# Writing the first quad's score stacks straight from the parts in an attention kernel

## The reference

```python
xn = _layernorm(x, axis=-1)
Q, K, V = split_heads(xn @ wq.T), split_heads(xn @ wk.T), split_heads(xn @ wv.T)   # 16 heads of 8 channels
Q, K = _rope(Q, THETA), _rope(K, THETA)
scores = jnp.einsum('bhqd,bhkd->bhqk', Q, K) / sqrt(8)      # causal mask, softmax
out = (softmax(scores) @ V) @ wo.T
x = x + out + (xn @ CB.T) * (SCB / 127) + bias
```

## Time and profile before

| | |
|---|---|
| median of 3 runs | 259.69 us (259.62 to 261.62) |
| the profiled execution's own time | 259.88 us |
| its span, first to last instruction | 258.2 us |
| TensorE busy | 240.1 us, 93% |
| VectorE busy | 218.7 us, 85% |
| ScalarE busy | 183.6 us, 71% |
| GpSimd busy | 103.6 us, 40% |
| mean DMA rate | 89 GB/s |

### The profile page before, as it was taken

One profiled execution on the slowest core, in us unless ns is written; L12 is line 12 of the kernel. 1 busy time (PEld: TensorE's weight loads), 2 busy tenths in 40 slices (PEclk: granted clock), 3 DMA queues, 4 the chain that ended last, 5 costly groups with the idle time before them and its releaser, 6 DMA issues.

```text
span 258.2 us, 10150 instructions
## 1 busy us (share of the span) xinstructions
PE 240.1 (93%) x4294; PEld 124.1 (48%) x4294; DVE 218.7 (85%) x594; ACT 183.6 (71%) x360; POOL 103.6 (40%) x169
## 2 busy tenths in 40 slices
PE   6888896888999999999999999999999999999945
PEld 6546541233344555554554465445555554436334
DVE  7899268999999999989999998999889989962072
ACT  2045732273997888779788878889889799999701
POOL 7570724749856391293233032304401430440300
PEclk9999998699999999999999999999999999999997
DMA  7625758620230467162027103700770210010602
GB/s 196 220 66 150 202 120 156 144 46 4 67 85 23 106 165 129 44 165 67 5 81 165 29 4 103 158 18 3 192 163 5 90 41 4 3 44 20 182 10 84
DMA packets 23559, 22.96 MB, mean 89 GB/s; under 512 B 2757, under 2 KB 20549, under 8 KB 23513
## 3 DMA queue, kind: packets, MB, share of 16 engines
q1 hardware_dynamic: 23368, 22.05, 34.3%
q10 hardware_dynamic: 144, 0.26, 0.4%
HBM read 13.70 MB, written 8.39 MB: 86 GB/s over the span
## 4 chain that ended last, share of the span: by engine, by line
PE 72%; DVE 13%; ACT 5%; DMA 4%; SPq 2%; issue 2%; POOL 1%; ACTq 0%
PE psA L918 22%; PE psB L918 20%; PE psV L990 18%; DVE prod L802 8%; ACT ring L697 3%; PE psB L906 2%; PE psB L901 2%; PE psA L1030 2%; DMA qs<-shiftsT 2%; SPq L384 2%; DMA rest<-o_scratch 2%; PE psA L872 1%; DVE rest L815 1%; PE psB L872 1%; ACT xnT L639 1%
## 5 line engine op out<-in xcount | busy, mean ns | idle before, releaser
L802 DVE CUSTOM_DVE_ANT_0 prod<-psA,cmask 128x128 f32<-128x128 f32 (+7 forms) x256 | 177.9, 754 | 16.7 <-PE psA L918 15.6
L697 ACT ACTIVATE ring<-psB 128x512 f32<-128x512 f32 x288 | 154.5, 608 | 33.6 <-PE psB L918 30.7
L918 PE MATMUL psB<-qs,ks 128*32 128x512 bf16 (+3 forms) x1536 | 99.2, 327 | 0.5 <-DMA qs<-shiftsT 0.2
L918 PE MATMUL psA<-ks,qs 128*32 128x512 bf16 (+3 forms) x1536 | 94.7, 334 | 5.3 <-DVE mx L802 4.5
L990 PE MATMUL psV<-ring,va 128*32 128x512 f32 (+3 forms) x768 | 76.0, 486 | 0.1
L918 PEld LDWEIGHTS psB<-qs,ks 128*32 128x32 bf16 x1536 | 40.8, 96 | 48.6 <-ACT ring L697 24.2
L559 POOL TENSOR_SCALAR_AFFINE_SELECT ring<-ring 128x512 f32<-128x512 f32 x64 | 40.0, 642 | 48.2 <-ACT ring L697 48.2
L918 PEld LDWEIGHTS psA<-ks,qs 128*32 128x32 bf16 x1536 | 34.2, 96 | 43.8 <-DVE mx L802 28.0
L539 POOL CAST shifts<-mx 128x16 bf16<-128x16 f32 x16 | 3.2, 198 | 71.0 <-DVE mx L802 71.0
L990 PEld LDWEIGHTS psV<-ring,va 128*32 128x32 f32 x768 | 22.5, 110 | 16.6 <-issue 8.9
L802 DVE DVE_READ_ACCUMULATOR2_ANT mx<- 128x1 f32 x256 | 21.3, 83 | 0.0
(11 more groups left out here) (89 smaller groups left out, 157.0 us busy)
## 6 DMA issues: line engine op xcount, KB each, us to landing
qs<-q_scratch SPq DMA_DIRECT2D x48, 96.0 KB
ks<-k_scratch SPq DMA_DIRECT2D x48, 96.0 KB
o_scratch<-ot SPq DMA_DIRECT2D x12, 256.0 KB, 2.6
q_scratch<-ot SPq DMA_DIRECT2D x20, 128.0 KB, 2.5
k_scratch<-ot SPq DMA_DIRECT2D x12, 128.0 KB, 2.5
x_sb<-x SPq DMA_DIRECT2D x4, 256.0 KB, 4.5
rope_sb<-rope SPq DMA_DIRECT2D x2, 512.0 KB, 6.8
rot<-o_scratch SPq DMA_DIRECT2D x3, 256.0 KB, 3.5
```

What stands on the lines that cost most here:

```text
L697: act.activation(ring[:, s % P_RING, k * HALF:(k + 1) * HALF], bank_b(e % B_RING), ACT.Exp)\
L802: last = dve.tensor_tensor_reduce(masked_scores[:, u % 2, at:at + w], psA[:, (u % 2) * SEQ + at:(u % 2) * SEQ + at + w], cmask[:, SEQ - w: ...
L918: mm = pe.matmul(psum[strip:strip + STRIP, at:at + size], keys[:, strip:strip + STRIP], queries, start=True, stop=True)
```

## The change

- Quad 0's stacks no longer go through HBM. SP issues, for each of the 12 parts of token halves 0 and 1, three DMAs from the part's first 32 partitions (in SBUF) to 8 rows each of the stack (in SBUF): 36 DMAs of 32 KB (`stack_part`). They stand ahead of everything else on SP after the inputs; the 16 stores of `store_parts(0)` and `store_parts(1)` come behind them, then the loads for quads 1 and 2.
- For that the channels are ordered by quad, then dimension, then head (the host permutes the weights' rows and the rope table), so that the 32 partitions of a quad, read in order, are 8 dimensions of 4 heads. The scratch tensors get the shape [quads, parts, dimension, head, tokens].
- Two tasks stand ahead of quad 0's first unit instead of five, and all 22 units of quad 0 stand ahead of bank 0. The third and the fourth group of four tiles of the normalised x are made on ACT (`normalise(2)`, `normalise(3)`) with a bias that POOL computes.
- ACT issues the two DMAs of quad 0's shifts itself. `load_stack(3)` moves between `store_shifts(1, 1)` and `store_parts(3)`.
- All tables are new.

```diff
-        scratch = (nc.dram_tensor("q_scratch", [HEADS, PARTS + 2, DH, BATCH * SEQ], BF16),
-                   nc.dram_tensor("k_scratch", [HEADS, PARTS, DH, BATCH * SEQ], BF16))
+        scratch = (nc.dram_tensor("q_scratch", [HEADS // QUAD, PARTS + 2, DH, QUAD, BATCH * SEQ], BF16),
+                   nc.dram_tensor("k_scratch", [HEADS // QUAD, PARTS, DH, QUAD, BATCH * SEQ], BF16))
...
-                    sp.dma_start(scratch[c % 2][:, m, :, tok:tok + HALF], part(c, n)).then_inc(scratch_out[c // 2], 16)
+                    sp.dma_start(scratch[c % 2][:, m, :, :, tok:tok + HALF], part(c, n)).then_inc(scratch_out[c // 2], 16)
...
-                                     source[heads, first:first + PARTS, :, tok:tok + HALF]
-                                     .rearrange("h p d t -> (p d) h t")).then_inc(ready, 16)
+                                     source[i % 4, first:first + PARTS, :, :, tok:tok + HALF]
+                                     .rearrange("p d h t -> (p d) h t")).then_inc(ready, 16)
...
+            def stack_part(c, n):
+
+                hf, stack = c // 2, (qs, ks)[c % 2]
+                if n < 2:
+                    sp.wait_ge((part1, part2)[n], c + 1)
+                else:
+                    sp.wait_ge(part3[c], 1)
+                for g in range(PARTS):
+                    row = g * GROUP + ((n - g) % PARTS if c % 2 == 0 else n) * DH
+                    sp.dma_start(stack[row:row + DH, 0, hf, :, :], part(c, n)[0:QUAD * DH, :]).then_inc(stack_in[0][hf], 16)
+
+            sp.wait_ge(pads0_ready, 2)
+            for n in range(PARTS):
+                for c in (0, 1):
+                    stack_part(c, n)
+            stack_part(2, 0)
+            stack_part(2, 1)
+            stack_part(3, 0)
+            stack_part(3, 1)
+            stack_part(2, 2)
+            stack_part(3, 2)
             store_parts(0)
-            sp.wait_ge(pads0_ready, 2)
-            sp.wait_ge(scratch_out[0], 16 * ROUND_DMAS)
-            load_stack(0, 0)
             store_parts(1)
+            sp.wait_ge(pads1_ready, 2)
+            sp.wait_ge(scratch_out[0], 16 * ROUND_DMAS)
+            load_stack(1, 0)
             sp.wait_ge(scratch_out[1], 16 * ROUND_DMAS)
-            load_stack(0, 1)
-            sp.wait_ge(pads1_ready, 2)
-            load_stack(1, 0)
             load_stack(1, 1)
-            store_shifts(0, 0)
             sp.wait_ge(pads2_ready, 2)
             load_stack(2, 0)
             load_stack(2, 1)
-            store_shifts(0, 1)
...
+            def first_leave(c):
+                pool.wait_ge(part1, c + 1)
+                pool.wait_ge(part3[c - 2], 1)
+                pool.tensor_tensor(rest[:, c % 2, :], rot[:, c % 2, :], part(c, 0), ALU.subtract).then_inc(rest1, 1)
...
+            def normalise(g):
+                act.wait_ge(shift_ready, g - 1)
+                for t in range(4 * g, 4 * g + 4):
+                    act.activation(xn[:, t, :], x_sb[:, t, :], ACT.Identity, bias=mean_shift[:, t:t + 1],
+                                   scale=rstd[:, t:t + 1]).then_inc(xn_late_ready, 1)
...
-PROJECT_BANK = [269, 276, 296]
-TURN_FIRST = 292
+PROJECT_BANK = [261, 271, 296]
+TURN_FIRST = 285
```

More of the change, by code:

```diff
@@ L435, in _ @@
                 if i == 1:
+                    sp.wait_ge(b_filled, ring_place(i, 0))
+                    load_stack(i + 2, 0)
+                    load_stack(i + 2, 1)
                     store_parts(3)
@@ L439, in _ @@
                         store_heads(done, hf)
-                if i + 2 < QUADS:
+                if 1 < i and i + 2 < QUADS:
                     if i == 2:
@@ L481, in _, with scales, mean_shifts @@
             pads(qs, 1, 0.0, pads1_ready)
-            for g in range(4):
+            def scales(g):
                 bt = slice(4 * g, 4 * g + 4)
-                pool.wait_ge(ln_step, 2 * g + 2)
-                pool.tensor_scalar(var_eps[:, bt], mv[:, bt, 1], EPS, None, ALU.add).then_inc(rstd_step, 1)
-                pool.wait_ge(rstd_step, g + 2)
+                pool.wait_ge(ln_step, 3 * g + 3)
+                pool.wait_ge(rstd_step, 1)
                 pool.tensor_tensor(rstd[:, bt], var_eps[:, bt], exponent[:, bt], ALU.pow).then_inc(rstd_ready, 1)
+            def mean_shifts(g):
+                bt = slice(4 * g, 4 * g + 4)
+                pool.wait_ge(rstd_ready, g + 1)
+                pool.tensor_tensor(mean_shift[:, bt], mv[:, bt, 0], rstd[:, bt], ALU.mult).then_inc(shift_step, 1)
+                pool.wait_ge(shift_step, g - 1)
+                pool.tensor_scalar(mean_shift[:, bt], mean_shift[:, bt], -1.0, None, ALU.mult).then_inc(shift_ready, 1)
+            scales(0)
+            scales(1)
+            scales(2)
+            mean_shifts(2)
             pool.memset(cmask[:, :], 0.0).then_inc(cmask_ready, 1)
@@ L604, in masks @@
                         copy_v(i, 1)
[L605 to L612, removed]
+                if i == 1 and 3 <= s < 7:
+                    add_ffn(s - 3)
+                if i == 2 and 3 <= s < 7:
+                    add_bias(s - 3)
+            beside(-3)
+            pads(qs, 2, 0.0, pads2_ready)
+            pads(ks, 2, TWO_MINUS_ONES, pads2_ready)
+            for n in (-2, -1):
                 beside(n)
@@ L666, in save_task @@
                 last.then_inc(task_saved, 1)
+            def normalise(g):
[3 more added lines that the diff above has]
+                                   scale=rstd[:, t:t + 1]).then_inc(xn_late_ready, 1)
             turned_rows(0)
+            parts_of(0, 0)
             turned_rows(1)
-            for n in range(2):
-                parts_of(0, n)
-                parts_of(1, n)
+            parts_of(1, 0)
+            parts_of(0, 1)
+            parts_of(1, 1)
+            normalise(2)
+            parts_of(2, 0)
             turned_rows(2)
+            parts_of(2, 1)
+            parts_of(3, 0)
             save_task(0)
+            parts_of(3, 1)
+            for n in range(1, ROWS3_FIRST):
+                save_task(n)
+            normalise(3)
             turned_rows(3)
[L676 to L681, removed]
+            for n in range(ROWS3_FIRST, len(TASKS)):
                 save_task(n)
@@ L743, in statistics @@
                 last.then_inc(ln_step, 1)
+                dve.wait_ge(ln_step, 3 * g + 2)
+                bt = slice(4 * g, 4 * g + 4)
+                dve.tensor_scalar(var_eps[:, bt], mv[:, bt, 1], EPS, None, ALU.add).then_inc(ln_step, 1)
             def normalise(g):
@@ L772, in rotate @@
                 cols = slice((r % 2) * HALF, (r % 2 + 1) * HALF)
-                dve.wait_ge(projected, c + 1)
-                for m in range(2):
-                    dve.tensor_tensor(prod[:, c % 2, m, :], round_bank(r, 2 * w + m), rope_sb[:, m, cols],
-                                      ALU.mult).then_inc(products, 1)
+                dve.wait_ge(projected, 2 * c + m + 1)
+                dve.tensor_tensor(prod[:, c % 2, m, :], round_bank(r, 2 * w + m), rope_sb[:, m, cols],
+                                  ALU.mult).then_inc(products, 1)
+            def rotate(c):
                 dve.wait_ge(products, 2 * c + 2)
@@ L781, in rotate, with third_part @@
                                   ALU.add).then_inc(rotated, 1)
-            rotate(0)
-            rotate(1)
+            def third_part(c):
+                dve.wait_ge(part2, c + 1)
+                dve.tensor_tensor(part(c, 2), rest[:, c % 2, :], part(c, 1), ALU.subtract).then_inc(part3[c], 1)
+            for c in (0, 1):
+                product(c, 0)
+                product(c, 1)
+                rotate(c)
             leave(0)
             leave(1)
-            normalise(2)
-            dve.wait_ge(part2, 2)
-            dve.tensor_tensor(part(1, 2), rest[:, 1, :], part(1, 1), ALU.subtract).then_inc(part3[1], 1)
-            normalise(3)
+            product(2, 0)
+            third_part(1)
+            product(2, 1)
             rotate(2)
+            product(3, 0)
+            product(3, 1)
             rotate(3)
-            leave(2)
-            leave(3)
+            statistics(3)
             def maximum(i, u):
```

119 lines of the change are left out of this document (71 added, 48 removed), and 30 rows, old and new, of tables (UNIT_BANK, VALUE_BANK).

## The result

The changed kernel takes **278.01 us** (median of 4 runs, 275.94 to 279.76), the kernel before 259.66: a ratio of 1.068, with an interval of 1.059 to 1.078. The forecast of 268.1 had the sign and the main cause, but less than half of the size: 18.3 us were lost, not 8.2, and the time lies above the range, which ended at 273. The profiled execution took 278.58 us.

What follows compares the result with a forecast made beforehand. TensorE's work was taken to bound the kernel from quad 1's unit 0 to the end of the values, with DVE setting quad 0's pace; 259.88 + 9.9 + 0.9 - 2.6 gave 268.1 us, range 255.5 to 273.

Steps and rivals of the forecast that it cites:

- Stores on four engines: 16 stores ahead of quad 1's loads: four engines, 49 ns per 1 KB, 1.57 us each, 25.1 us in all.
- Rival (b): Stores keep 16 engines: 255.9 us (chance 0.12), or 248.7 us with cheap issues too (chance 0.08).
- (a): Stores on four engines, but the new stack DMAs issue like loads, 0.38 us: 260.9 us; chance 0.20.
- Issue of the new DMAs: Quad 0's stack DMAs on SP: 0.60 us each plus 0.04 between, 36 taking 23.0 us, SP through at 37.7.
- Quad 1's unit 0: First unit of quad 1, behind the stores and six loads: issued at 67.2 us, 9.9 later than at 57.27.
- part three: Everything besides quad 1's unit 0: +0.9 us for work left over, -2.6 in the tail, 0 for shifts and later stores.
- up to 1 us: Stores of rounds 2 and 3: 0, or up to 1 us if the shift of quad 1's second half comes late.
- Half clock after the wait: TensorE returns at half clock after waiting more than 10 us, for up to 6.9 us: +3.4 us at most.
- rival (c): Worse than the forecast: stores at 60 ns a packet, +6.1, so 274 us, or TensorE at half clock; chance 0.10.
- Part one: Start and quad 0: 36 new DMAs, first 640-wide maximum at about 39.8 us, later tasks hidden by DVE's units.
- part two: Stores ahead of quad 1's loads: on four engines, last store at 64.8 us, quad 1's unit 0 at 67.2.
- Tail: After the last value step: quad 7's first-half save stands at bank 18 instead of 23, -2.6 us.

Runs made afterwards that it cites:

- pair of runs above: Changed kernel with its stores on sixteen engines, 260.95 us (ratio 1.006); kernel before with its stores on four engines, 276.09 us (1.064).
- the run with the old pattern: Changed kernel, its stores still on four engines, with loads of stacks reading the scratch in the order of the kernel before: 284.86 us (1.098).
- stores16: Changed kernel with each store going to 128 consecutive scratch rows, so on sixteen engines (also called the sixteen-engine version): 260.95 us (1.006).

## Why the prediction was wrong, step by step

- **Stores on four engines: right.** 80 GB/s and a share of 0.25 were forecast, 96 and 0.27 measured. One packet took 46 ns where 49 were taken (32 × 49 = 1.57 us a store; the sixteen went from 40.1 to the first load that waits for them, at 64.58, in 24.5 us where 27.1 were forecast). The pair of runs above makes the shape alone 16 to 17 us. Rival (b), sixteen engines, is ruled out. (It is also the case meant where the prediction writes "with 16 the sum would be the first rival's": (a) has four engines.)
- **Issue of the new DMAs: right in kind, a little low.** 0.71 for each and not 0.64; SP was through at 40.1 instead of 37.7. Rival (a), at the loads' price, was far off.
- **Quad 1's unit 0: 67.2 forecast, 69.33 measured.** +2.4 from the issues, -2.6 from the stores, and +2.3 from the loads: 2.4 us had been priced by packet counts at 49 ns, and 4.75 us passed between 64.58 and 69.33. The dearer issue of a load isn't the reason, as the run with the old pattern had unit 0 at 68.84. That the number came within 2.1 us is in part luck: misses of both signs.
- **The step that failed** is in part three: "the shifts of quad 0 on ACT's queue ... end long before they are wanted, under the waits above: 0", with the stores of rounds 2 and 3 at "0, with up to 1 us". The stage from quad 1's unit 0 to quad 2's bank 0 was to grow by 0.9 and grew by 11.3. Of this 2.1 us are the work left over (stores16), and 9.2 go with the four-engine stores. Within the 9.2, waits for shift DMAs are 4.9 us of TensorE's idle time, and TensorE's busy time is 52.7 against 48.3 us for the same matmuls: 4.4 us at the lower clock, granted 0.92 on average. The prediction asked which wait ends last at unit 0, and then took everything behind it as the work that it was before. But the late stores had moved quad 1's and quad 2's loads onto the very stretch in which quad 0's second shift is sent, and the shift's packets moved only 3.4 us after its issue, behind them (2.5 us of TensorE's idle time). The next wait, 2.1 us at 106, is the one that "up to 1 us" stood for: the shift is issued at 100.19, behind the last three stores of a round, and lands 5.94 later. That both waits come from the stores' shape is shown by the sixteen-engine version, which has neither; that the second is due to those three stores is my reading.
- **Half clock after the wait** was rival (c)'s: "+3.4 at most". The 4.4 above are of that kind. It isn't a case apart, but comes with the waits: with 9 us of an idle TensorE the granted clock is 0.54 on average over 62.9 to 73.1 us, which is mostly the level of 1.2 GHz; in the sixteen-engine version, without the waits, it is 1.00 throughout the stage.
- **Part one had the later tasks "hidden by DVE's units": they aren't.** In the version without the stores' wait, from the first 640-wide maximum to quad 1's unit 0 pass 18.0 us (42.2 to 60.3), and 17.2 when the stack comes early (31.9 to 49.0, granted clock 1.00). Before it was 15.2 (42.05 to 57.27). TensorE is the one that is full there, not DVE:

```profile
41.70:60.30 18.60, 18.42 (x189) 9.02 (x189) 14.90 (x31) 5.57 (x11) 10.27 (x9) 0.91 0.50 165
```

  Seven tasks among the units cost 2 to 3 us. In the changed kernel this lay beneath the stores' wait, as the prediction said of part two; its rival (b) had unit 0 at 55.0, and of the 5.3 us to the 60.3 that was measured this is about half, the later start (42.2 for 39.8) the rest.
- **Tail: right in mechanism, low in size.** -4.4 us in the changed kernel, and 3.1 us of the whole time in the kernel before (ratio 0.988), against -2.6.

Summed in the prediction's terms: +12.1 for +9.9, +11.0 for +0.9 (11.3 less 0.3), and -4.4 for -2.6.

What stays open is the stretch of the loads' packets to 125 ns, and whether a layout exists that serves quad 0 with few DMAs and lets the stores keep sixteen engines; the sixteen-engine versions here permute the rows of the scratch tensors, and such a layout wasn't tried. Sixteen engines alone wouldn't do: with 36 DMAs on SP those stores only bring back the time before.

## What to carry to other kernels

When a change makes transfers late, price the next stage as well: list every small transfer issued while the late ones drain, and count what was issued ahead of it, by other engines too. Look at the outermost size of each DMA that a new layout touches, on both sides, before anything else: here 4 in place of 16 cost 16 to 17 us, where all the other edits together moved the time by 1.3. And an issue made cheaper is no gain by itself; issuing sooner what isn't urgent puts it ahead of what is.

## What the runs showed of the hardware

- The same load of 24 × 4 rows of 1 KB takes SP 0.376 or 0.758 us to issue, by the order of its rows in HBM alone, in both kernels.
- A DMA from 32 partitions to 8, SBUF to SBUF, takes mostly 0.65 to 0.67 us to issue, and the next one starts about 0.04 behind it.
- A shift DMA of 32 rows of 256 B on two engines lands in 2.0 us with little ahead of it, and in 6.1, 8.6 and 12.9 us among the loads for quads 1 and 2. Its packets start 0.9, 3.4 and 9.4 us after the issue in the runs with 2.0, 6.1 and 12.9: a DMA issued by ACT waits behind what SP issued earlier.
- A 1 KB packet of a load takes about 54 ns where SP's pace sets the rate and 73 ns in a backlog at 162 GB/s; where the loads were issued behind stores on four engines it takes about 125, at 105 GB/s. Packets of the stores themselves take 46 ns with four engines always busy.
- With four engines taking what SP issues, the issue of a store stretches from 0.56 to about 1.3 us, the time that a store's 128 KB need at their 96 GB/s.
